# Query columns in another DRAM layout, one load per step in place of two, and a new drawing of the order

## The reference, cut to what matters

```python
x = x + 0.5 * ffn(layernorm(x))     # "job" (1, b) for sequence b
x = x + attention(layernorm(x))
x = x + 0.5 * ffn(layernorm(x))     # "job" (2, b)
```

```python
k_val = causal_conv4(x @ W_mem)[:, :256]                   # (t, K, HH)
p     = exp(clip(scale * s) + log_w)                       # (t, K)
state = cumsum(p * exp(i * k_val * theta)) / cumsum(p)     # (t, K, HH, M), complex
q     = x @ W_q                                            # (t, KQ, HH, M, 2)
out   = sum over M of state * conj-like products with repeat(q, 8)
y     = out_re @ W_re + out_im @ W_im ; y_val * silu(y_gate) ; @ W_out
```

## Time and profile before

| | |
|---|---|
| time, median of 3 runs | 1193.39 us (1191.97 to 1195.2) |
| time of the profiled execution | 1190.12 us |
| its span in the trace | 1188.9 us |
| PE busy | 1024.6 us (86%) |
| DVE busy | 729.8 us (61%) |
| ACT busy | 631.0 us (53%) |
| POOL busy | 487.2 us (41%) |
| DMA engines, mean rate | 145 GB/s |

### The profile page before, as it was taken

How to read it: one execution, slowest core, us unless ns; L and a number is a source line. 1 busy time by engine, 2 the same in 40 slices (tenths; PEclk the granted TensorE clock), 3 DMA queues, 4 the chain that set the end, 5 groups by cost and what they waited for, 6 DMA issues and landing times.

```text
span 1188.9 us, 11370 instructions
## 1 busy us (share of the span) xinstructions
PE 1024.6 (86%) x3424; PEld 569.3 (48%) x3424; DVE 729.8 (61%) x1210; ACT 631.0 (53%) x1090; POOL 487.2 (41%) x451
## 2 busy tenths in 40 slices
PE   5987989888879979979499989898987899989993
PEld 2465635555344444435255534445453554436661
DVE  2310116878889989879679888998998931200000
ACT  4343325648556588355366574436778852224451
POOL 3434451454553334532432231534363523155642
PEclk9988999998999989989799899898998999999997
DMA  9876571657864666873565757246687645426757
GB/s 311 325 245 158 78 168 49 154 135 159 169 170 105 166 164 109 182 197 107 141 154 117 187 118 178 60 123 180 108 199 164 145 67 77 110 66 130 122 94 113
DMA packets 68977, 172.54 MB, mean 145 GB/s; under 512 B 12354, under 2 KB 12354, under 8 KB 66790
## 3 DMA queue, kind: packets, MB, share of 16 engines
q0 software_dynamic: 32576, 72.44, 33.9%
q1 hardware_dynamic: 36342, 99.38, 27.6%
HBM read 112.86 MB, written 68.33 MB: 152 GB/s over the span
## 4 chain that ended last, share of the span: by engine, by line
PE 29%; DMA 23%; DVE 16%; issue 12%; POOL 11%; ACT 7%; SPq 1%; POOLq 0%; DVEq 0%; ACTq 0%
PE hps L887 8%; PE yps L903 7%; DMA xs<-x_normal,rows_i 4%; DMA x_rows<-ys,rows_i 3%; DMA q_cols<-xin 3%; PE misc L965 3%; DMA xin<-in_x 3%; DVE run L1474 2%; PE xps L878 2%; PE yps L845 2%; DMA qx<-q_cols 2%; PE misc L931 2%; POOL slots L1660 2%; DVE trig L1481 2%; DMA xin<-sum_rows 2%
## 5 line engine op out<-in xcount | busy, mean ns | idle before, releaser
L887 PE MATMUL hps<-w_all,hidden_sb 128*128 x848 | 215.0, 399 | 16.5 <-ACT hidden_sb L1069 13.6
L1674 POOL DMA_INDIRECT xs<-x_normal,rows_i x106 | 128.3, 1210 | 227.8 <-PE xps L878 169.2
L903 PE MATMUL yps<-w_all,hidden_sb 128*128 x424 | 207.8, 614 | 5.7 <-ACT hidden_sb L1069 5.7
L887 PEld LDWEIGHTS hps<-w_all,hidden_sb 128*128 128x128 f32 x848 | 164.5, 201 | 58.1 <-issue 38.4
L1474 DVE TENSOR_TENSOR_SCAN run<-pwx,trig 128x512 f32<-128x512 f32 x128 | 149.5, 1210 | 23.8 <-ACT trig L1157 15.9
L1698 POOL DMA_INDIRECT x_rows<-ys,rows_i x56 | 96.0, 1714 | 118.7 <-ACT ys L1082 112.4
L833 PE MATMUL hps<-xnT,sw_sb 128*128 128x512 f32 x256 | 117.9, 610 | 9.2 <-ACT hidden_sb L1042 9.2
L845 PE MATMUL yps<-sw_sb,hidden_sb 128*128 128x512 f32 x256 | 121.6, 619 | 0.0
L1082 ACT ACTIVATE ys<-yps,slots 128x512 f32<-128x512 f32 x106 | 73.0, 689 | 89.8 <-PE yps L903 72.5
L878 PE MATMUL xps<-ident,xs 128*128 128x128 f32 x424 | 69.7, 292 | 54.5 <-DMA xs<-x_normal,rows_i 25.9
L903 PEld LDWEIGHTS yps<-w_all,hidden_sb 128*128 128x128 f32 x424 | 80.7, 198 | 74.5 <-issue 71.0
(11 more groups left out here) (202 smaller groups left out, 1530.4 us busy)
## 6 DMA issues: line engine op xcount, KB each, us to landing
qx<-q_cols SPq DMA_DIRECT2D x128, 256.0 KB
w_all<-in_w_experts SPq DMA_DIRECT2D x8, 1024.0 KB, 10.2
x_normal<-xin SPq DMA_DIRECT2D x32, 256.0 KB, 4.2
xin<-x_rows SPq DMA_DIRECT2D x32, 256.0 KB, 7.1
turns_sb<-in_w_out SPq DMA_DIRECT2D x3, 1536.0 KB, 11.5
xin<-in_x SPq DMA_DIRECT2D x16, 256.0 KB, 6.2
sum_rows<-ys SPq DMA_DIRECT2D x16, 256.0 KB, 5.7
xin<-sum_rows POOLq DMA_DIRECT2D x16, 256.0 KB, 8.4
```

The lines of the kernel that those rows point to most:

```text
L887: t = PE.matmul(hps[:, bank, 0:H], xT[:, j % 2, c, :], w_all[:, bass.ds(expert[j] + c * H, H)], start=c == 0, stop=c == KC - 1)
L903: t = PE.matmul(yps[:, bank, :], hb[:, j % 2, ec, :], w_all[:, bass.ds(expert[j] + (KC * H + ec * D), D)], start=ec == 0, stop=ec == EC - 1)
L1674: GE.indirect_dma_start(xs[:, j % NX, :], None, xn_rows[PAIR_OF[g]], bass.IndirectOffsetOnAxis(rows_i[:, g % 2, j:j + 1], 0)).then_inc(*xs ...
```

## The change

The layout of the queries in DRAM becomes (2, half, angle m, group in half, head, re/im, t). The store of one query group still moves 128 rows of 2 KB (256 KB), but the slowest dimension of its DRAM access pattern is now 16 (head and re/im), where it was 2. The two loads of a step (256 KB each, with the 8-fold repeat over keys as the slowest dimension) become one load of 512 KB for all 128 partitions, whose slowest dimension is 16 (group and head) with the repeat behind it. For that, keys and heads stand on partitions as head * 8 + key within a quarter, so the weights, the taps, theta, norm and the block-diagonal matrices are laid out anew on the host, and `rep_sb` is made by one select for each copy instead of two. The order is drawn anew: the assumed costs of the inverse root (3.6 to 5.2) and of the load's issue (1.2 to 0.7) change, `URGENT` is replaced, and two tables are added, `PARTS` by part of the kernel and `KINDS` by engine and stage.

```diff
-        q_dram = nc.dram_tensor("q_cols", (2, KQ, M, HH, 2, T), F32)
+        q_dram = nc.dram_tensor("q_cols", (2, HALVES, M, QH, HH, 2, T), F32)
...
-            piece("POOL", ("load", q), 3.6, ("DVE", ("load", q)))
+            piece("POOL", ("load", q), 3.6 if q < 2 else 5.2, ("DVE", ("load", q)))
...
-            piece("POOL", ("a_stats", b), 3.6, ("DVE", ("a_stats", b)))
+            piece("POOL", ("a_stats", b), 5.2, ("DVE", ("a_stats", b)))
...
-            piece("SP", ("c_query", b, n), 1.2, *[("SP", ("a_q", b, half * QH + g), 2.5) for g in range(QH)], *free)
+            piece("SP", ("c_query", b, n), 0.7, *[("SP", ("a_q", b, half * QH + g), 2.5) for g in range(QH)], *free)
...
+        PARTS = {"job": {1: -212, 6: -255},
+                 "blocks": {1: -66, 3: 151},
+                 "head": {1: -279},
+                 "tail": {0: 179, 1: 458, 2: -285},
+                 "steps": {0: -813}}
+        KINDS = {("ACT", "a_q"): -350,
+                 ("ACT", "c_turn"): -567,
+                 ("ACT", "mid"): -1222,
+                 ("ACT", "o_rows"): 346,
+                 ("ACT", "two"): -1557,
+                 ("ACT", "x"): 59,
+                 ("DVE", "a_fall"): 119,
+                 ("DVE", "c_scan"): 2680,
+                 ("DVE", "c_turn"): 144,
+                 ("PE", "a_mem"): 932,
+                 ("PE", "a_spread"): 650,
+                 ("PE", "a_turn"): 985,
+                 ("PE", "acc"): 170,
+                 ("PE", "c_out"): 203,
+                 ("PE", "gT"): 2158,
+                 ("PE", "logits"): 275,
+                 ("PE", "mid"): 840,
+                 ("PE", "one"): -62,
+                 ("PE", "turn"): -2672,
+                 ("PE", "two"): 231}
...
+        def urgency(k):
+
+            engine, stage, at = k[0], k[1][0], k[1][1] if len(k[1]) > 1 else 0
+            return (URGENT.get((engine, stage), {}).get(at, 0.0) + KINDS.get((engine, stage), 0.0)
+                    + PARTS.get(PART_OF.get(stage), {}).get(at, 0.0))
...
-                GE.memset(rep_sb[:, :], 1.0).then_inc(*consts.of(7))
+                GE.memset(rep_sb[:, :], 0.0).then_inc(*consts.of(7))
...
-                    GE.affine_select(out=reps_i, in_=reps_i, compare_op=ALU.is_ge, fill=0.0, base=0,
-                                     pattern=[[1, KH]], channel_multiplier=-HH).then_inc(*consts.of(10 + i))
+                    GE.affine_select(out=reps_i, in_=reps_i, compare_op=ALU.not_equal, fill=1.0, base=0,
+                                     pattern=[[KPQ, KQ], [0, HH], [1, KPQ]], channel_multiplier=-1).then_inc(*consts.of(10 + i))
...
-                for i, reps_i in enumerate(reps):
-                    pool.wait_ge(*consts.at(13 + i))
-                    GE.affine_select(out=reps_i, in_=reps_i, compare_op=ALU.is_ge, fill=0.0, base=HH - 1,
-                                     pattern=[[-1, KH]], channel_multiplier=HH).then_inc(*consts.of(14 + i))
...
-                SP.dma_start(bass.AP(q_dram, (b % 2 * KQ + q) * P * T, [[T, 2], [2 * T, M * HH], [1, T]]),
-                             xin[:, q, :]).then_inc(*q_stored[q].of(b))
+                half, g = divmod(q, QH)
+                into = bass.AP(q_dram, ((b % 2 * HALVES + half) * M * QH + g) * HH * 2 * T,
+                               [[T, 2 * HH], [QH * HH * 2 * T, M], [1, T]])
+                SP.dma_start(into, xin[:, q, :]).then_inc(*q_stored[q].of(b))
...
-                for g in range(QH):
-                    q = b % 2 * KQ + half * QH + g
-                    src = bass.AP(q_dram, q * P * T + m * HH * 2 * T, [[0, KPQ], [2 * T, HH], [1, 2 * T]])
-                    SP.dma_start(qx[g * KPQ * HH:(g + 1) * KPQ * HH, s, :, :], src).then_inc(*q_loaded[s].of((b, n, g)))
+                src = bass.AP(q_dram, ((b % 2 * HALVES + half) * M + m) * QH * HH * 2 * T,
+                              [[2 * T, QH * HH], [0, KPQ], [1, 2 * T]])
+                SP.dma_start(qx[:, s, :, :], src).then_inc(*q_loaded[s].of((b, n)))
```

More of the change, by code:

```diff
@@ L494, in plan_tail @@
                 piece("POOL", s, 1.0, ("ACT", s), ("POOL", ("m_rows", b), 10.0))
-        URGENT = {
[L497 to L525, removed]
-        }
@@ new lines, in macaron @@
+        PART_OF = {name: part for part, names in (
+            ("job", "fetch load norm turn chunks logits rank gates gT hidden acc"),
+            ("blocks", "place scatter slots rows bring x one mid two add"),
+            ("head", "w_head a_load a_add m_rows a_stats a_norm a_turn a_mem a_p a_fall a_den a_q a_spread"),
+            ("tail", "w_tail c_out o_gate o_mul o_rows o_sum"),
+            ("steps", "c_count c_query c_turn c_scan c_times c_sum")) for name in names.split()}
+        PARTS = {"job": {1: -212, 6: -255},
[3 more added lines that the diff above has]
+                 "steps": {0: -813}}
@@ new lines, in macaron @@
+        URGENT = {
+            ("ACT", "one"): {0: 631},
+            ("ACT", "two"): {1: 1845},
+            ("DVE", "c_out"): {0: -88},
+            ("DVE", "c_sum"): {2: -749},
+            ("DVE", "c_times"): {1: 115, 3: -81},
+            ("DVE", "c_turn"): {1: -55, 2: 91},
+            ("DVE", "gates"): {5: 241},
+            ("PE", "a_q"): {2: -352, 3: -83},
+            ("PE", "a_spread"): {2: 356},
+            ("PE", "acc"): {2: -167},
+            ("PE", "c_out"): {0: -267},
+            ("PE", "hidden"): {2: 116, 5: -165, 6: -13},
+            ("PE", "o_gate"): {2: 300, 3: 1079},
+            ("PE", "one"): {1: 53, 4: 425},
+            ("PE", "place"): {1: -42, 2: 65},
+            ("PE", "two"): {1: -540, 3: 346},
+            ("PE", "x"): {3: -118, 5: -425},
+        }
@@ L548, in orders @@
                     way[k] -= 10000.0
-                way[k] += URGENT.get((k[0], k[1][0]), {}).get(k[1][1] if len(k[1]) > 1 else 0, 0.0)
+                way[k] += urgency(k)
             free, table, begun, ended, made = {}, None, {k: 0.0 for k in work}, {}, {}
@@ L682, in macaron @@
         y_kept = signal("s_y_kept", BV)
-        consts = signal("s_consts", range(16))
+        consts = signal("s_consts", range(14))
         chunk_sums = signal("s_chunk_sums", range(2))
@@ L712, in macaron @@
         q_stored = [signal(f"s_q_stored{q}", range(B), 16) for q in range(KQ)]
-        q_loaded = [signal(f"s_q_loaded{i}", [(b, n, g) for b, n in BN if n % 2 == i for g in range(QH)], 16)
+        q_loaded = [signal(f"s_q_loaded{i}", [(b, n) for b, n in BN if n % NQX == i], 16)
                     for i in range(NQX)]
@@ L1479, in real_products @@
                 vec.wait_ge(*scanned.at((b, n)))
-                vec.wait_ge(*q_loaded[n % NQX].at((b, n, QH - 1)))
+                vec.wait_ge(*q_loaded[n % NQX].at((b, n)))
                 VE.tensor_tensor(trig[:, n % 2, :, :], run[:, :, :], qx[:, n % NQX, :, :],
@@ L1541, in soften @@
                 if i == 0:
-                    vec.wait_ge(*consts.at(15))
+                    vec.wait_ge(*consts.at(13))
                     vec.wait_ge(*small_loaded.at(2))
@@ L1805, in pool_program @@
                     more_tables()
-                    own = consts.at(15)
+                    own = consts.at(13)
                 elif stage == "scatter":
@@ L1999, in laid_out, with by_head @@
     small[:, 0:SC] = sb1.reshape(SC, P).T
-    taps = conv_k[:, 0, :].T
+    KPQ = K // 4
+    def by_head(a):
+        rest = a.shape[1:]
+        return a.reshape(K // KPQ, KPQ, HH, *rest).swapaxes(1, 2).reshape(K * HH, *rest)
+    taps = np.concatenate([by_head(conv_k[:, 0, :].T[:K * HH]), conv_k[:, 0, :].T[K * HH:]])
+    w_mem = np.concatenate([by_head(w_mem[:, :K * HH].T).T, w_mem[:, K * HH:]], axis=1)
     for i in range(2):
@@ L2003, in laid_out @@
     small[K:2 * K, SC + 8:SC + 12] = taps[2 * P:]
-    small[:, SC + 12:SC + 28] = theta.reshape(2, P, M).transpose(1, 0, 2).reshape(P, 2 * M)
-    small[:, SC + 28:SC + 30] = norm.reshape(2, P).T
+    small[:, SC + 12:SC + 28] = by_head(theta.reshape(K * HH, M)).reshape(2, P, M).transpose(1, 0, 2).reshape(P, 2 * M)
+    small[:, SC + 28:SC + 30] = by_head(norm.reshape(K * HH)).reshape(2, P).T
     small[K:2 * K, SC + 30] = scale
@@ L2013, in laid_out @@
     KQ = w_q.shape[1] // (2 * M * HH)
-    w_q = w_q.reshape(D, KQ, HH, M, 2).transpose(0, 1, 4, 3, 2).reshape(D, KQ * 2 * M * HH)
+    w_q = w_q.reshape(D, KQ, HH, M, 2).transpose(0, 1, 2, 4, 3).reshape(D, KQ * 2 * M * HH)
     W = 8 * NV
@@ L2024, in laid_out @@
                 for vg in range(2):
-                    full[vg, part * 64 + kk * HH:part * 64 + (kk + 1) * HH, kk * NV:(kk + 1) * NV] = \
+                    full[vg, part * 64 + kk:part * 64 + 64:8, kk * NV:(kk + 1) * NV] = \
                         w[8 * g + kk][:, vg * NV:(vg + 1) * NV]
```

2 lines of the change are left out of this document (1 added, 1 removed).

## The result

The changed kernel takes 1148.81 us (median of 4 runs, 1146.13 to 1150.35) against 1193.32 us (4 runs) before. The ratio is 0.9641, with a 95% interval of 0.9607 to 0.9675, so it is 44.5 us faster. One run each of experiments 9 and 13 fell in a slower state of the chip and is left out of their times, all others are fast runs. The forecast was 1177 us, with a range from 1157 to 1197. The direction was right, the size was not: nearly three times the 15.8 us of the sum.

What follows compares the result with a forecast made beforehand. No engine was taken to bound the whole; PE's idle time could be won. Terms 2.2 + 1.95 + 10.6 + 1 summed to 15.8 us, and 1193.4 - 15.8 gave 1177 us, range 1157 to 1197.

Steps and rivals of the forecast that it cites:

- What bounds the kernel: No engine bounds the whole; PE's 105 us of idle time in the attention steps (195 to 960 us) can be won.
- The stores: Query stores, on two engines at 51 GB/s, would land in 4.2 us: 5.1 us shorter alone, 16 us for the pile's last.
- the pile: Four query stores issued together before the third sequence; DVE's 10.60 us wait at 577 us goes, leaving PE a 7 us gap.
- the clock: PE's clock fell to 1.2 GHz after the gap at 577 us; a shorter gap returns 0 to 2 us, 1 taken.
- The loads: A step's query load on 16 engines gets 1.95 us shorter, or 0.6 us if other traffic fills the unused engines.
- The sum on DVE: DVE's shortened waits for query loads and for rows behind query stores, at six places from 218 to 577 us: 24 us.
- the first four places: DVE's waits at 218, 256, 280 and 350 us, forecast to shrink by 3.50, 5.1, 1.8 and 1.95 us.
- What of it reaches the end: Of DVE's 24 us, PE gains 2.2 at 250 to 260, 1.95 at 341 to 350, 10.6 at 577 us, plus 1 for clock.
- Edits at nothing: POOL's removed select (0.85 us for two, covered by a wait), the new key order and the planner's assumed costs: nothing.
- The order: The planner's redrawn instruction order: taken as 0, bounded by one longest gap, 17.6 us more or less.
- turns last make it slower: Rival: `turn` last on PE delays seven `xin` handovers by 3.60 us each, 25 us, so 1202 us; chance 0.13.
- the order gives more: Rival: the new order removes one more longest gap from PE's idle time, 17.6 us, so 1160 us; below 1165, chance 0.14.

Runs made afterwards that it cites:

- experiment 9: New layout with the old order, but each step's load split into two 256 KB DMAs with slowest dimension 16: 1144.34 us, ratio 0.9584 to the kernel before.
- experiment 13: Kernel before with old stores, query loads left out, products from a constant tile in one buffer (control with DVE's self-waits): 1150.61 us, ratio 0.9661.
- Experiment 5: New layout with the old order, plus eight more scans (9.7 us) on DVE at about 215 us: 1158.86 us, ratio 0.9738 to the kernel before.
- experiment 12: Kernel before with old stores and eight-engine loads, but loads go to a buffer DVE never reads, products from a constant tile: 1186.36 us, ratio 0.9946.
- experiment 8: New layout and spread store with the old order, no query loads, products from a constant tile: 1140.67 us, ratio 0.9568 to the kernel before.
- experiment 1: All of the change except the planner's hunks, so new layout, store and load in the old order: 1149.68 us, ratio 0.9661 to the kernel before.

## Why the prediction was wrong, point by point

- **What bounds the kernel**: that PE's idle time of the middle stage is what can be won is right (39.5 us of the 105 went). The sentence that a wait taken from DVE "counts in full only where PE stands still for the same reason" is wrong. Experiment 5 added 10 us to DVE where PE was full, and PE was 10 us later within 100 us; and of the lead of 40.1 us at 822 us, 37.9 reached the end.
- **The stores**: right in the main. Two engines for each store, 4.2 us forecast after the change and 2.9 seen; the pile at 577 us is gone and PE's gap of 7 us behind it came out as written. As an edit by itself the store was forecast at 13.8 us with the clock, and measured at 24 (14 to 29). But stores do not stand in line behind each other alone. In the trace before, SP issues two query loads at 542.01 us and the two stores of the earlier trace rows at 543.64:

```profile
542.01 1.19 SPq L1882 DMA_DIRECT2D qx<-q_cols  x2
...
544.00:547.00 3.00, 3.00 (x8) 1.33 (x7) 1.68 (x4) 1.18 (x2) 0.00 (x0) 1.00 0.53 141
...
548.00:550.00 2.00, 2.00 (x7) 0.90 (x6) 1.96 (x4) 0.79 (x2) 1.61 (x1) 1.00 0.12 47
```

  While the loads run, half of the engines are busy, not the ten that eight for the loads and two for a store would make, and the share of a store alone appears only behind them. So the stores stand behind the loads too, some 3 to 4 us here. The prediction read the pile as four stores in a line, 20.6 us against 20.19 seen; that these agree is luck.
- **The loads**: this is the first step that failed. They were priced by the time that a step waited for its own load (1.95 us at two or three places). The runs showed that DVE need not wait for them at all: loads that it never reads cost 35 us on eight engines beside the old store (experiment 12 against 13), and about 10 us on sixteen beside the new one. The prediction read the share of 0.51 in the earlier trace rows as a load that is half as fast as it could be. It should have read it as half of the engines being occupied for every other transfer too. The parts of stores and loads are not separate: of the 50 us between the kernel before and experiment 8, the spread store alone takes 24 and leaving out the loads alone takes 40, which is more than 50 together. At 544 us the trace shows stores held up by loads. That the busiest engines set the landings of rows and gathers too is inferred from these runs. The profile has no row for a single DMA engine.
- **The sum on DVE**, 24 us: close at the first four places, 6 us low at the pile and 16 us low at 822 us, since it named places where a query transfer stood last. The list of all waits of the kernel before for rows and queries would have been the better start. These rows of it were not used in the prediction:

```profile
DVE stats_ffn L1237 <- DMA xin<-x_rows: 15.7, 5, 10.6
DVE stats_ffn L1237 <- DMA xin<-in_x: 14.4, 9, 6.4
...
DVE stats_attn L1390 <- DMA xin<-sum_rows: 8.2, 10, 2.5
DVE trig L1481 <- DMA qx<-q_cols: 8.0, 3, 3.5
```

  They are 46.3 us. In the trace of experiment 1 the same four are left with 9.2, and none of it is for `qx`:

```profile
DVE stats_ffn L1237 <- DMA xin<-in_x: 5.1, 4, 3.5
DVE stats_attn L1390 <- DMA xin<-sum_rows: 2.6, 4, 1.1
DVE stats_ffn L1237 <- DMA xin<-x_rows: 1.5, 2, 0.9
```

  The difference, 37.1 us, is nearly the whole 37.9 us between the spans. That they agree so closely is partly chance: in experiment 12 the same waits are 10.8 us less than before and the span is the same (1189.0 us), and in experiment 13 they are 32.6 us less and the span is 43.6 us shorter.
- **What of it reaches the end**: the second step that failed. "At 218 and 280 us PE has no free time, so what DVE gains there is slack": PE was 20.2 us ahead at 551.82, where the sum had 4.15. All 24 in place of 15.8 out of 24 would have given 1169 us.
- **Edits at nothing**: the select and the new key order are part of experiment 1. No run sets them apart.
- **The order**: zero was right on the new transfers (1148.8 against 1149.7 us), and that is luck: the same order costs 25 us on the old ones, and other orders on the new ones lie up to 49 us higher. The rival "turns last make it slower" did not occur; taking that entry out cost 25 us. The rival "the order gives more" had the time on its side of 1165 us, but the order gave nothing.
- **The rule of the Trainium skill** that the prediction weighed ("DMA: Bandwidth & Descriptors", "Rules for kernel authors", two transfers to disjoint halves) is half right here. Merging is worth nothing (experiment 9, 1144.3 us for two loads against 1149.7 for one). But the two halves did not share all sixteen engines, only eight. The Trainium skill, "DMA: Bandwidth & Descriptors", section "Why a DMA increments its semaphore by 16 and not by 1", says that the slowest dimension of each access pattern decides how many engines a DMA uses. The trace agrees: shares of 0.13 for a dimension of 2 and 0.51 for one of 8.

## What to carry to other kernels

Price a transfer not only by who waits for it, but by what it does to the engines that it sits on: 33.5 MB of loads on half the engines, beside stores on two, cost 35 us while neither DVE nor PE waited for them. Look at the slowest dimension of each access pattern, and look at the waits for all DMAs, not only those of the tensor that is changed. Where two engines run locked in-order streams, do not call a microsecond slack because the other engine is busy: here 10 of 10 us added to DVE came through, and 7 of 10 added to PE. And an order drawn by a planner depends on its costs: change a cost or a transfer, and compare with the old order before you trust the new one.

## What the runs showed of the hardware that was not expected

A load that uses all sixteen engines is not twice as fast as one on eight. In the changed kernel two loads of 512 KB are the only transfers of the program from about 201 to 205 us:

```profile
201.00:202.00 1.00, 1.00 (x5) 0.87 (x5) 0.96 (x3) 0.89 (x2) 0.00 (x0) 1.00 0.87 291
202.00:203.00 1.00, 1.00 (x6) 0.89 (x5) 0.96 (x2) 1.00 (x1) 0.00 (x0) 1.00 1.10 250
203.00:204.00 1.00, 1.00 (x4) 0.44 (x3) 0.96 (x2) 0.99 (x3) 0.00 (x0) 1.00 1.00 221
204.00:205.00 1.00, 1.00 (x3) 0.29 (x2) 0.97 (x2) 1.00 (x3) 0.00 (x0) 1.00 1.02 238
```

The rate is 221 to 291 GB/s, where eight engines moved 193, not the 386 of the prediction's estimate, although nearly every engine is busy (the profile's share can pass 1). So in this stretch a load moves 15% to 50% faster, not twice as fast. On eight engines the rate was not fixed either: 141 GB/s from 544 to 547 us, shown above. That the gain of the change lies more in the balance over the engines than in the load's own time fits experiment 12, and is not shown by itself.
